# Layer 0's product from two single-pass parts, and a new hand-out of the quantisation levels

## What is computed

```python
# layer 0: a long convolution over the 512 features of each token position (32 kernels), then a product
y = irfft(rfft(kernel, n=1024) * rfft(u_masked, n=1024))[..., :512] + u_masked * D   # masked by length
w = weight_fp8.astype(x.dtype) * weight_scale            # 512 x 512, fp8 values times one scale
x = x + einsum('bsd,od->bso', y * mask, w)
# layer 1: one of 16 adapter matrices per sequence, then a gated unit with quantised weights
z = einsum('bij,bkj->bik', x, weight[adapter_ids])
dq1, dq2, dq3 = (nf4_quant_dequant(w) for w in (w1, w2, w3))   # blocks of 64, 16 values, hidden size 1376
x = x + einsum('bsh,dh->bsd', silu(z @ dq1.T) * (z @ dq2.T), dq3)
# layers 2 and 3: low-rank experts, a small memory with top-8, a gate, a dense layer (not touched)
```

## Time and profile before

| | us |
|---|---|
| median of 3 runs | 896.24 (896.14 to 896.71) |
| the profiled execution | 897.49 |
| its span on the core | 895.7 |
| PE busy | 854.5 (95%) |
| DVE busy | 617.3 (69%) |
| ACT busy | 410.6 (46%) |
| the granted clock of PE, tenths | 9 (90% or more) in each of 40 slices |

### The profile page before, as it was taken

One profiled execution on the slowest core, in us unless ns is written; L12 is line 12 of the kernel. 1 busy time (PEld: TensorE's weight loads), 2 busy tenths in 40 slices (PEclk: granted clock), 3 DMA queues, 4 the chain that ended last, 5 costly groups with the idle time before them and its releaser, 6 DMA issues.

```text
span 895.7 us, 10638 instructions
## 1 busy us (share of the span) xinstructions
PE 854.5 (95%) x3287; PEld 461.3 (51%) x3288; DVE 617.3 (69%) x964; ACT 410.6 (46%) x530; POOL 155.6 (17%) x174
## 2 busy tenths in 40 slices
PE   0599999999999999999999999999999999999998
PEld 0497448999444444444444444444455554543443
DVE  7798998887888888899998836163262552457535
ACT  5124647886887777877868710000011232253100
POOL 6300008810112121222103210001401022020000
PEclk9999999999999999999999999999999999999999
DMA  6796237551000001101000110005020000002022
GB/s 180 247 322 232 82 118 261 191 212 67 24 23 19 6 18 33 33 0 33 33 1 0 34 57 1 0 0 188 0 66 1 0 1 1 1 1 47 11 83 94
DMA packets 34873, 60.98 MB, mean 68 GB/s; under 512 B 6056, under 2 KB 8696, under 8 KB 34184
## 3 DMA queue, kind: packets, MB, share of 16 engines
q1 hardware_dynamic: 34040, 60.26, 19.5%
q0 software_dynamic: 704, 0.10, 0.3%
q10 hardware_dynamic: 80, 0.01, 0.0%
HBM read 50.84 MB, written 8.47 MB: 66 GB/s over the span
## 4 chain that ended last, share of the span: by engine, by line
PE 91%; DVE 3%; issue 2%; POOL 2%; ACT 1%; DMA 0%; SPq 0%; POOLq 0%; ACTq 0%; DVEq 0%
PE ps L945 89%; PE ps L1003 1%; PE ps L1272 1%; DVE acc L1565 1%; DVE W2T L1426 1%; DMA T<-kpad 0%; DVE X L1908 0%; POOL lan_i L654 0%; ACT Yp L877 0%; PE ps L1306 0%; DVE Yp L1578 0%; PE ps L1229 0%; SPq L536 0%; POOL gsc L649 0%; POOL kk L649 0%
## 5 line engine op out<-in xcount | busy, mean ns | idle before, releaser
L753 ACT ACTIVATE above<-raw,cst 128x1024 bf16<-128x1024 f32 (+2 forms) x225 | 272.4, 1235 | 120.3 <-DVE acc L1565 44.6
L1565 DVE SCALAR_TENSOR_TENSOR acc<-above,acc 128x1024 f32<-128x1024 bf16 (+2 forms) x112 | 151.3, 1351 | 25.6 <-ACT above L753 21.6
L945 PE MATMUL ps<-Yp,W3T 128*128 (+2 forms) x746 | 159.7, 368 | 3.1 <-DVE Yp L1578 1.6
L945 PE MATMUL ps<-Up,W2T 128*128 128x512 f32 (+1 forms) x404 | 160.6, 593 | 0.0
L945 PE MATMUL ps<-Up,W1T 128*128 128x512 f32 x344 | 155.4, 594 | 0.1
L1565 DVE SCALAR_TENSOR_TENSOR T<-above,T 128x1024 f32<-128x1024 bf16 (+1 forms) x84 | 118.1, 1406 | 22.7 <-ACT above L753 19.5
L945 PEld LDWEIGHTS ps<-Yp,W3T 128*128 128x128 f32 x746 | 103.5, 191 | 54.8 <-issue 51.9
L945 PEld LDWEIGHTS ps<-Up,W2T 128*128 128x128 f32 (+1 forms) x404 | 66.5, 177 | 85.9 <-issue 85.6
L945 PEld LDWEIGHTS ps<-Up,W1T 128*128 128x128 f32 x344 | 64.3, 190 | 79.1 <-issue 76.3
L945 PE MATMUL ps<-X,W3T 128*128 128x512 f32 (+2 forms) x184 | 78.5, 578 | 0.0
L945 PE MATMUL ps<-X,W2T 128*128 128x512 f32 x140 | 61.3, 594 | 0.0
(11 more groups left out here) (338 smaller groups left out, 882.7 us busy)
## 6 DMA issues: line engine op xcount, KB each, us to landing
W3T<-in_wa SPq DMA_DIRECT2D x8, 1024.0 KB, 5.4
raw<-in_w SPq DMA_DIRECT2D x20, 256.0 KB, 3.0
W3T<-kpad SPq DMA_DIRECT2D x9, 512.0 KB, 6.5
Up<-in_xconv SPq DMA_DIRECT2D x4, 1024.0 KB, 11.9
X<-in_xT SPq DMA_DIRECT2D x4, 1024.0 KB, 8.7
W1T<-in_wa SPq DMA_DIRECT2D x4, 1024.0 KB, 5.8
xkeep<-X SPq DMA_DIRECT2D x4, 1024.0 KB, 4.7
X<-xkeep SPq DMA_DIRECT2D x4, 1024.0 KB, 9.2
```

The costliest lines, as they stand in the source:

```text
L753: nc.scalar.activation(above[0:h, m % 2, 0:w], raw[0:h, u % 2, 0:w], ACT.Relu, scale=STEEP, bias=cst[0:h, C_BND + i:C_BND + i + 1]).then_i ...
L945: return nc.tensor.matmul(o, l, r, start=start, stop=stop, **kw)
L1565: V.scalar_tensor_tensor(out=ac, in0=src, scalar=float(STEPS[i]), in1=ac, op0=ALU.min, op1=ALU.add).then_inc(s["m_used"], 1)
```

## The change

- Layer 0's product is made of two matmuls where there was one: `Yhi` is y rounded to the format f32r, `Ylo` is the remainder y - Yhi, in f32r too, and the weights `w0r` are in f32r. Both go into the same PSUM bank. An f32 matmul leaves two records in the trace; a row of an f32r matmul is not in this trace.
- `conv_out(g)` writes to one of four small buffers (`ytmp`) in the order of PSUM. ACT makes `Yhi` from it, and after that DVE makes `Ylo` (`conv_rest`, behind `conv_out` of the next group). The parts lie under `Yp` and `Up`, `w0r` under `W3T`.
- The product's tokens stay in the order position, sequence. So a block of 512 tokens needs a quarter of the convolution's groups, and PE waits for these by `a_hi` and `d_lo` in place of all of `d_conv`. The evacuation of a tile puts the tokens into X's order: it reads PSUM with a step of 64 elements, and writes pieces of 8 elements.
- Each tile now holds a part of all sequences, so X can be saved only after the last tile. The four `keep` go to the adapter stage, one behind each of the loads of adapters 4 to 7.
- The levels: 5 in the convolution (was 10), 7 in the product (26), 56 in the adapter stage (50), 97 in the first 24 tiles of up (79 in 21), 60 in the last 20 (60 in 21). Units 0 and 1 are transposed in the adapter stage.
- PE reads the bounds of the adapters from `order` in the convolution in place of the product.

```diff
-        w0 = w3f[:, 0:2048].rearrange("p (c o) -> p c o", c=DC)
+        ytmp = [w1f[:, 1024 + i * 512:1024 + (i + 1) * 512].rearrange("p (c n) -> p c n", c=DC) for i in range(4)]
...
-        NCV, NF0, NAD = 10, 26, 50
-        UP_A, UP_B = 21, 21
+        NCV, NF0, NAD = 5, 7, 56
+        UP_A, UP_B = 24, 20
...
-        K_CONV = [min(max(g - 4, 0), NCV) for g in range(HG)]
-        K_FFN0 = [NCV + min(2 * (n + 1), NF0) for n in range(TB * DC)]
+        K_CONV = [min(max(g - 4, 0) // 2, NCV) for g in range(HG)]
+        K_FFN0 = [K_CONV[-1] + (NF0 + NCV - K_CONV[-1]) * (n + 1) // (TB * DC) for n in range(TB * DC)]
...
             def keep(tb):
-                sp.wait_ge(s["d_x1"], (tb + 1) * DC)
+                sp.wait_ge(s["d_x1"], TB * DC)
...
-                keep(tb)
...
                 load_adapter(a)
-                if a == NWS:
-                    keep(TB - 1)
+                if NWS <= a < NWS + TB:
+                    keep(a - NWS)
...
+            for g in range(HG):
+                for k in parts_of(K_CONV, g):
+                    level(k)
+                act.wait_ge(s["d_conv"], g + 1)
+                nc.scalar.activation(Yhi[:, :, g * GH * NB:(g + 1) * GH * NB], ytmp[g % 4], ACT.Copy).then_inc(s["a_hi"], 1)
...
-            pe.wait_ge(s["d_conv"], HG)
             pe.wait_ge(s["d_w0"], 1)
-            pe.wait_ge(s["d_ord"], 1)
-            bounds = []
             for n in range(TB * DC):
                 tb, oc = n // DC, n % DC
                 if n >= len(BANKS0):
                     pe.wait_ge(s["d_x1"], n - len(BANKS0) + 1)
+                else:
+                    pe.wait_ge(s["d_conv"], HG - len(BANKS0) + 1 + n)
+                pe.wait_ge(s["a_hi"], HG // TB * (tb + 1))
                 for c in range(DC):
-                    last = mm(ps[:, BANKS0[n % len(BANKS0)], :], w0[:, c, oc * P:(oc + 1) * P], Y[:, c, tok(tb)], c == 0, c == DC - 1)
+                    if c == 0:
+                        pe.wait_ge(s["d_lo"], HG // TB * (tb + 1))
+                    for part in (Yhi, Ylo):
+                        last = mm(ps[:, BANKS0[n % len(BANKS0)], :], w0[:, c, oc * P:(oc + 1) * P], part[:, c, tok(tb)],
+                                  c == 0 and part is Yhi, c == DC - 1 and part is Ylo)
                 last.then_inc(s["p_ffn0"], 1)
...
-                V.tensor_tensor(Y.rearrange("p c (b s) -> p c s b", s=S)[:, :, g * GH:(g + 1) * GH, :],
+                V.tensor_tensor(ytmp[g % 4].rearrange("p c (k b) -> p c k b", k=GH),
                                 ps[:, g % 6, :].rearrange("p (c k b) -> p c k b", c=DC, k=GH),
...
+            def conv_rest(g):
+
+                cols = slice(g * GH * NB, (g + 1) * GH * NB)
+                dve.wait_ge(s["a_hi"], g + 1)
+                V.tensor_tensor(Ylo[:, :, cols], ytmp[g % 4], Yhi[:, :, cols].bitcast(f32), ALU.subtract).then_inc(s["d_lo"], 1)
...
                 dve.wait_ge(s["p_ffn0"], n + 1)
-                V.scalar_tensor_tensor(out=X[:, oc, tok(tb)], in0=ps[:, BANKS0[n % len(BANKS0)], :], scalar=wsc[:, 0:1],
-                                       in1=X[:, oc, tok(tb)], op0=ALU.mult, op1=ALU.add).then_inc(s["d_x1"], 1)
+                place = X[:, oc, :].rearrange("p (b s) -> p b s", s=S)[:, :, tb * S // TB:(tb + 1) * S // TB]
+                V.scalar_tensor_tensor(out=place, in0=ps[:, BANKS0[n % len(BANKS0)], :].rearrange("p (s b) -> p b s", b=NB),
+                                       scalar=wsc[:, 0:1], in1=place, op0=ALU.mult, op1=ALU.add).then_inc(s["d_x1"], 1)
```

48 lines of the change are left out of this document (25 added, 23 removed).

## The result

The changed kernel takes **903.38 us** (median of 4 runs, 902.90 to 905.32) against 896.48 for the kernel before beside it: a ratio of 1.0076, 95% interval 1.0055 to 1.0098. It is slower by 0.8%, and outside the forecast range of 881 to 900. The profiled execution is the one of 902.90 us, span 901.1; before it was 897.49 and 895.7, so 5.4 us are to be explained.

A forecast was written before the change was run, and what follows sets the result against it. PE was taken as the bound, with ACT and DVE's chain of levels close behind. Of 29.9 us saved in layer 0, 4.2 stay: 896.24 - 4.2 = 892.0 us; range 881 to 900, the forecast's own 888 to 896.

The forecast's parts named there:

- What bounds the kernel: Whole run: PE is the bound, with a second chain over ACT and DVE 13.5 us behind it at most.
- Parts 1 and 2: PE's product and DVE's work up to there: 0.215 us a matmul, product ends at 107.5, layer 0 29.9 us earlier.
- C: Layer 0's evacuation pays for its steps on both sides, 1.29 us each, so DVE bounds the product: 898.9 us; chance 0.10.
- D: Layer 0's product: f32r is no faster a record than f32, so it takes 54.9 us as before: 919 us; chance 0.06.
- Part 3, the chain of levels: Behind layer 0: 24 more levels cost 38.1 us, chain ends at 521.9, 6.9 later; 4.2 us of gain left.
- Nothing behind it changes: From down on: DVE's sums for down are covered by PE's first 19 us of down, so no time changes there.
- Part 4, the saves: Four saves of X among the loads of adapters 4 to 7: rows 0 to 3 us late, 0 taken.
- E: Unit rows land late between the saves, or scalings and starts cost more where POOL works: 895 to 899 us; chance 0.10.
- B: ACT and DVE shed their waits for PE when PE is ahead: 868 us in full, up to 886 in part; chance 0.12.

The follow-up runs named there:

- e1: The kernel before, its f32 product kept, with the changed kernel's hand-out of levels (12 done by the product's end instead of 36): 930.1 us.
- e12: The changed kernel with 20 levels by the product's end, 54 in the adapter stage and up's levels in 23 and 19 tiles: 898.5 us.
- e4: The changed kernel with the levels of the four rest-column tiles (28, 29, 32, 33) put behind their own work on ACT and DVE: 901.5 us.
- e8: The changed kernel, saving and restoring only 32 of each 512 tokens of X, with the DMAs, order and waits kept: 901.4 us.
- e17: The changed kernel with 20 instead of 12 levels by the product's end, ACT's convolution levels one group ahead, 50 in the adapter stage: 889.3 us.
- e18: e17 with matmuls nobody reads in three PE waits: ahead of the first adapter, tile 30 and the last unit's turn: 887.5 us.

## Why the prediction was wrong

**What bounds the kernel**: right. The second chain was named with its distance, and it is what took the gain.

**Parts 1 and 2**: right. A matmul was forecast at 0.215 us and takes 0.228; the product ended at 107.95 (forecast 107.5) and `d_x1` at 109.00 (108.6). That the ends agree so well is luck in part: the product took 29.15 us and not 27.5, but it began at 78.80 and not at 80.0. An evacuation takes 0.66 to 0.67 us from start to start, the low end of the bounds, which the sum had used, and not the 0.75 that the text then takes; rivals C and D are out. The sentence from the Trainium skill (SBUF — State Buffer, Door 1) that spoke for C is not borne out on the read side here: with a step of 256 bytes in PSUM, DVE is as fast as it was without. The penalty stands there for SBUF, and for PSUM only with matmuls; the prediction carried it over to DVE's reads. The convolution's pair of groups with a level, forecast at 5.0 us, takes 4.88, with the wait of 1.14 in it.

**Part 3, the chain of levels: the step that failed.** Its mechanism is right: the chain sets down's start, and the last unit is exposed for 1.63 + 2.4 us, which is the 4.0 measured (4.0 to 4.5 in every run that has its last level in tile 43 and no fillers there). The term that was mis-sized is the price of the 24 more levels. From the end of `d_x1` to the end of the last scaling the forecast was 521.9 - 108.6 = 413.3 us, measured 528.7 - 109.0 = 419.7. The 24 more levels were put at 1.26 us each and, with starts and scalings, at 38.1, and the waits were said to change little; e1 shows 43.0, in a kernel without any of the other edits. The 1.26 is DVE's time for a level, and DVE's work was priced well: its busy time in the chain grew by 36.8 us. What is missing is the waits. DVE's idle time in the chain grew from 50.9 to 57.3 us, by 6.4, in step with the levels (0.27 us each), where the forecast took 1.3 us away. The kernel before already had a price with the waits in it: 373.5 us for 189 levels, 1.98 each, starts and scalings included, against 38.1/24 = 1.59 in the sum and 1.79 measured. The changed kernel's ACT from 109 to 204 us (busy, mean ns of one; idle before, and for whom):

```profile
L758 ACT ACTIVATE above<-raw,cst 128x1024 bf16<-128x1024 f32 x52 | 58.3, 1145 | 14.4 <-DVE acc L1573 5.3 <-DVE W2T L1573 3.3 <-DVE T L1573 3.2
L797 ACT ACTIVATE Up<-ps x22 | 13.1, 597 | 7.1 <-ACT Up L797 5.8 <-issue 0.8 <-PE ps L952 0.5
```

While PE waits 8.0 us for ACT's adapter copies, ACT itself stands 7.1 us at these copies, mostly between one group and the next, with levels queued behind them, and 14.4 ahead of its levels, most of it for DVE. The gaps are not slack: in a fixed order each of the three waits for the others at some time, and four levels more in this stage cost 7.2 us of it (e12). PE's waits came out near the 22 us that the text has: 22.0 in the rows above, without the 2.4 at the adapters' start. But the places that the text gives for them, 6, 4 and some 5, add up to only 15 or so, and the 22 measured lie otherwise: 8.0 in the adapter stage (forecast 6), 3.6 at tile 2 (4), 1.6 in tiles 3 to 24 (some 5), 5.5 at tile 30, which was not forecast, and 3.3 around the last unit's turn. The working counted the tiles with rest columns like the others, though DVE's multiplication stands behind the levels there; with that order turned round (e4) this wait was gone, and 3.8 of its 5.5 us came back elsewhere.

**The clock** had no term. It cost 3.0 us, in down's first stretch, 22.04 for 19.05; "Nothing behind it changes" is the sentence that failed. Before, PE hardly waited and the clock was at its level throughout; the change made the waits.

**Part 4, the saves**: the sum took 0 and the range 3; e8 puts them at up to 2 us, and e1, with the saves in their old place, has a chain only 0.2 us shorter than the changed kernel's. A save took 11.7 us to land and not 4.7, among the adapters' loads.

Forecast to measured on the profiled runs: 893.3 + 0.4 (`d_x1`) + 6.4 (the chain) + 3.0 (the clock) - 0.2 = 902.9. Of the rivals, E's late rows are there, but with 0.8 us of DVE's waits and at most 2 us in all they are less than the 3 to 7 us that E gave them, and not the cause. B, an elastic chain, is refuted by e1, where 24 levels cost their 43 us in full. The forecast's own range of 888 to 896 left the chain's waits little room on the upper side: 4 us, where 24 levels at 1.26 to 1.8 us alone differ by 13.

What the change was worth in itself: with the hand-out mended (e17) it is 0.9% faster than before, with fillers (e18) 1.1%. e17's last scaling is at 515.2 us, against 513.4 before: 16 more levels behind the product, 29.3 us at 1.83 each, have used up the 27.5 us that layer 0 gives. The gain is the spare time that lay between the last scaling and down, 15.2 us before and 4.0 now, less the 1.8 by which the scaling is later and the 2.8 of the lower clock.

## What to carry to other kernels

When a stage is shortened that hid other work, price that work by the chain it then stands in, waits included: take two points of the same chain (here 374.7 us for 189 levels and 417.7 for 213, 1.79 for one more), not the busy time of one engine. Such a price holds as a mean over many levels and does not say what two or four of them do at one place. Before handing work on to later stages, look for room in the shortened one, and ask which small order (ACT's level behind its copy) closes it. Reordering within late tiles moved waits about for 0 to 2 us; eight levels moved ahead gave 14. Ending a hidden chain earlier in the order is no gain by itself: with its last step two tiles earlier the chain ended at nearly the same time, and one more tile of PE's work stood behind it.
